# The last projection of a recurrent block in three fp32r passes on twelve of sixteen chunks, with low parts made by GpSimd

## What is computed

```
xn = layernorm(x)                                   # over the 256 values
A  = sigmoid(log_A);  Bx = xn @ B_w.T + B_b
h_t = A * h_(t-1) + Bx_t                            # along the 1024 tokens of a sequence
s  = h @ C_w.T + C_b
y  = sum over the top 2 of 8 experts of  c_e * (silu(xn @ W1_e) * (xn @ W3_e)) @ W2_e
out = x + s * silu(y)
```

## Time and profile before

| | |
|---|---|
| median of 3 runs | 799.54 us (797.96 to 799.91) |
| the profiled execution | 799.78 us, its span 798.0 us |
| PE busy | 771.4 us, 97% of the span |
| DVE, ACT, POOL busy | 518.2, 375.1, 463.8 us |
| share of the chain that ended last | PE 84%, DVE 8% |

### The profile page before, as it was taken

One profiled execution on the slowest core, in us unless ns is written; L12 is line 12 of the kernel. 1 busy time (PEld: TensorE's weight loads), 2 busy tenths in 40 slices (PEclk: granted clock), 3 DMA queues, 4 the chain that ended last, 5 costly groups with the idle time before them and its releaser, 6 DMA issues.

```text
span 798.0 us, 17126 instructions
## 1 busy us (share of the span) xinstructions
PE 771.4 (97%) x5399; PEld 688.8 (86%) x5399; DVE 518.2 (65%) x1083; ACT 375.1 (47%) x665; POOL 463.8 (58%) x477
## 2 busy tenths in 40 slices
PE   4999989999999999999999999999999999999997
PEld 2554449999999999999999999999999999998786
DVE  6988965676777667666866564455556765552766
ACT  3975234454455345444544553445445654442530
POOL 4742847687476766856783687476547856544000
PEclk9999999999999999999999999999999999999999
DMA  9999913544565545435543644363537555943994
GB/s 291 330 302 334 131 41 107 125 77 67 127 141 113 101 81 106 68 53 135 138 70 96 165 61 79 42 145 60 112 67 192 98 128 101 329 66 40 307 373 165
DMA packets 101842, 111.02 MB, mean 139 GB/s; under 512 B 15634, under 2 KB 89236, under 8 KB 101748
## 3 DMA queue, kind: packets, MB, share of 16 engines
q0 software_dynamic: 25920, 35.54, 27.4%
q1 hardware_dynamic: 50032, 50.34, 20.3%
q10 hardware_dynamic: 25796, 24.20, 10.4%
HBM read 66.61 MB, written 43.45 MB: 138 GB/s over the span
## 4 chain that ended last, share of the span: by engine, by line
PE 84%; DVE 8%; DMA 2%; issue 2%; ACT 2%; ACTq 0%; POOL 0%; DVEq 0%; POOLq 0%; SPq 0%
PE bank L1506 15%; PE bank L1505 15%; PE bank L1507 15%; PE bank L1531 15%; PE bank L1532 7%; PE bank L1638 6%; PE bank L1494 3%; DVE xnT L1084 3%; PE bank L1406 2%; DVE stats L955 1%; PE bank L1369 1%; DVE xnT L1096 1%; PE bank L1557 1%; PE bank L1558 1%; PE bank L1556 1%
## 5 line engine op out<-in xcount | busy, mean ns | idle before, releaser
L605 POOL DMA_INDIRECT y_rows<-y_sb,token_at x128 | 215.5, 1684 | 150.8 <-DVE y_sb L1202 84.4
L1505 PE MATMUL bank<-xh,W_sb 128*128 128x256 f32 x1008 | 283.1, 281 | 1.2 <-DVE xl L1150 1.2
L1506 PE MATMUL bank<-xh,W_sb 128*128 128x256 f32 x1008 | 281.8, 280 | 0.0
L1507 PE MATMUL bank<-xl,W_sb 128*128 128x256 f32 x1008 | 281.7, 279 | 0.0
L1505 PEld LDWEIGHTS bank<-xh,W_sb 128*128 128x128 f32 x1008 | 189.2, 188 | 3.4 <-issue 1.3
L1531 PE MATMUL bank<-W_sb,hh 128*128 128x512 f32 x512 | 189.0, 408 | 0.7 <-DVE y_sb L1202 0.7
L1506 PEld LDWEIGHTS bank<-xh,W_sb 128*128 128x128 f32 x1008 | 189.4, 188 | 0.0
L1507 PEld LDWEIGHTS bank<-xl,W_sb 128*128 128x128 f32 x1008 | 188.9, 187 | 0.0
L1190 DVE TENSOR_TENSOR hbuf<-hbuf,bank 128x512 f32<-128x512 f32 x128 | 87.3, 686 | 148.8 <-PE bank L1507 129.5
L596 POOL DMA_INDIRECT xg<-xn_rows,token_at x128 | 145.3, 1136 | 37.8 <-issue 18.3
L1532 PE MATMUL bank<-W_sb,hl 128*128 128x256 f32 x512 | 143.9, 281 | 0.0
(11 more groups left out here) (253 smaller groups left out, 939.1 us busy)
## 6 DMA issues: line engine op xcount, KB each, us to landing
x_late<-L_attn_x SPq DMA_DIRECT2D x24, 512.0 KB, 9.2
raw<-L_ffn_W ACTq DMA_DIRECT2D x24, 512.0 KB
odd_raw<-L_ffn_W ACTq DMA_DIRECT2D x21, 512.0 KB
xn_rows<-h_sb SPq DMA_DIRECT2D x16, 512.0 KB, 7.4
y_rows<-xnT SPq DMA_DIRECT2D x4, 2048.0 KB, 16.2
yy<-y_rows SPq DMA_DIRECT2D x16, 512.0 KB, 9.3
out<-x_late SPq DMA_DIRECT2D x11, 512.0 KB, 6.6
x_kept<-L_attn_x SPq DMA_DIRECT2D x4, 512.0 KB, 6.9
```

What stands on the lines that cost most here:

```text
L605: return eng.indirect_dma_start(out=y_rows, out_offset=rows, in_=y, in_offset=None, bounds_check=T + TW - 1, oob_is_err=True, compute_op=A ...
L1505: eng.matmul(part, high, x_h, start=k == 0, stop=False)
L1506: eng.matmul(part, low, x_h, start=False, stop=False)
L1507: last = eng.matmul(part, high, x_l, start=False, stop=k == KD - 1)
```

## The change

Chunks 4 to 15 (`SPLIT_FROM` = 4) no longer use f32 matmuls. Their states are split in a part rounded to fp32r (`h_high`) and the rest (`h_low`), and so is the matrix (`CwT_high`, `CwT_low`); three fp32r matmuls of 256 columns (high by high, high by low, low by high) take the place of each f32 matmul. `h_high`, `h_low` and `h_sb` share one stretch of SBUF: the high part of chunk c is written where the states of chunk c-4 stood, so it waits until `states_out(c-4)` is done; the low part is written over the chunk's own states. ACT makes the high parts (Copy, 128 x 1024), POOL the low parts (a subtract, 128 x 1024, after its last scatter), DVE the low part of the matrix. On ACT the high parts of chunks 4, 5 and 6 stand ahead of the first silu, that of 7 behind the silu of chunk 0, and those of 8 to 15 behind the silus of 4 to 11. The load of the first chunk of y and its silu are cut in two halves.

```diff
+        with ExitStack() as split:
+            h_high = sb("h_high", [P, BATCH * KN * SEQ], f32r, split)
+        with ExitStack() as split:
+            h_low = sb("h_low", [P, BATCH * KN * SEQ], f32r, split)
         h_sb = sb("h_sb", [P, BATCH * KN * SEQ], f32)
...
+        SPLIT_FROM = len(S_BANKS)
+        def split_home(c):
+            home = c - SPLIT_FROM
+            return h_half(home // 2 * 2, home % 2, h_high)
...
             for c in range(CHUNKS):
-                eng.dma_start(yy[:, c, :].rearrange("p (t d) -> p t d", t=CT), y_v[:, c * CT:(c + 1) * CT, :]).then_inc(y_loaded[c], 16)
+                yy_c, y_c = yy[:, c, :].rearrange("p (t d) -> p t d", t=CT), y_v[:, c * CT:(c + 1) * CT, :]
+                if c == 0:
+                    eng.dma_start(yy_c[:, 0:2, :], y_c[:, 0:2, :]).then_inc(y_first_half, 16)
+                    eng.dma_start(yy_c[:, 2:4, :], y_c[:, 2:4, :]).then_inc(y_loaded[c], 16)
+                else:
+                    eng.dma_start(yy_c, y_c).then_inc(y_loaded[c], 16)
...
+            for c in range(SPLIT_FROM, CHUNKS):
+                eng.wait_ge(hs_high, c - SPLIT_FROM + 1)
+                eng.tensor_tensor(h_half(c // 2 * 2, c % 2, h_low), h_half(c // 2 * 2, c % 2), split_home(c).bitcast(f32),
+                                  ALU.subtract).then_inc(hs_low, 1)
...
+            def split(c):
+                eng.wait_ge(s_psum, 2 * (c - SPLIT_FROM) + 2)
+                eng.activation(split_home(c), h_half(c // 2 * 2, c % 2), ACT.Copy).then_inc(hs_high, 1)
+            eng.wait_ge(CwT_ready, 1)
+            eng.activation(CwT_high[:, :], CwT[:, :], ACT.Copy).then_inc(CwT_high_ready, 1)
+            for c in range(SPLIT_FROM, 2 * SPLIT_FROM - 1):
+                split(c)
             for c in range(CHUNKS):
-                eng.wait_ge(y_loaded[c], 16)
-                eng.activation(yy[:, c, :], yy[:, c, :], ACT.Silu).then_inc(g_ready, 1)
+                if c == 0:
+                    eng.wait_ge(y_first_half, 16)
+                    eng.activation(yy[:, c, 0:512], yy[:, c, 0:512], ACT.Silu).then_inc(g_ready, 1)
+                    eng.wait_ge(y_loaded[c], 16)
+                    eng.activation(yy[:, c, 512:1024], yy[:, c, 512:1024], ACT.Silu).then_inc(g_ready, 1)
+                    split(2 * SPLIT_FROM - 1)
+                else:
+                    eng.wait_ge(y_loaded[c], 16)
+                    eng.activation(yy[:, c, :], yy[:, c, :], ACT.Silu).then_inc(g_ready, 1)
+                if SPLIT_FROM <= c < CHUNKS - SPLIT_FROM:
+                    split(c + SPLIT_FROM)
...
+            eng.wait_ge(CwT_high_ready, 1)
+            eng.tensor_tensor(CwT_low[:, :], CwT[:, :], CwT_high[:, :].bitcast(f32), ALU.subtract).then_inc(CwT_low_ready, 1)
...
+                if c >= SPLIT_FROM:
+                    if c == SPLIT_FROM:
+                        eng.wait_ge(CwT_low_ready, 1)
+                    eng.wait_ge(hs_low, c - SPLIT_FROM + 1)
...
+                            else:
+                                high, low = split_home(c)[:, m, tokens], h_half(c // 2 * 2, c % 2, h_low)[:, m, tokens]
+                                eng.matmul(o, high, CwT_high[:, of], start=False, stop=False)
+                                eng.matmul(o, high, CwT_low[:, of], start=False, stop=False)
+                                last = eng.matmul(o, low, CwT_high[:, of], start=False, stop=ends and m == KN - 1)
```

More of the change, by code:

```diff
@@ L147, in build @@
             CwT = sb("CwT", [P, KN * D], f32, tail)
-            pad_to_weights = sb("pad_to_weights", [P, W_COLS - 2 * KN * D - 3 * D - P], f32, tail)
+            CwT_high = sb("CwT_high", [P, KN * D], f32r, tail)
+            CwT_low = sb("CwT_low", [P, KN * D], f32r, tail)
+            pad_to_weights = sb("pad_to_weights", [P, W_COLS - 4 * KN * D - 3 * D - P], f32, tail)
             yy = sb("yy", [P, CHUNKS, CT * D], f32, tail)
@@ L311, in build, with h_half @@
         y_loaded = [sem(f"y_loaded{c}") for c in range(CHUNKS)]
+        y_first_half = sem("y_first_half")
         s_psum = sem("s_psum")
+        CwT_high_ready, CwT_low_ready = sem("CwT_high_ready"), sem("CwT_low_ready")
+        hs_high, hs_low = sem("hs_high"), sem("hs_low")
         g_ready, u_ready, out_ready = sem("g_ready"), sem("u_ready"), sem("out_ready")
         out_stored = sem("out_stored")
-        def h_half(g0, q):
-            return h_sb[:, bass.ds(g0 * SEQ, KN * SEQ)].rearrange("p (m s) -> p m s", m=KN)[:, :, q * CW:(q + 1) * CW]
+        def h_half(g0, q, of=h_sb):
+            return of[:, bass.ds(g0 * SEQ, KN * SEQ)].rearrange("p (m s) -> p m s", m=KN)[:, :, q * CW:(q + 1) * CW]
+        SPLIT_FROM = len(S_BANKS)
+        def split_home(c):
+            home = c - SPLIT_FROM
+            return h_half(home // 2 * 2, home % 2, h_high)
         def wait_apart(eng, semaphore, value):
@@ L1334, in add_x @@
                 eng.tensor_tensor(x_g, yy[:, c, at:at + cols], x_g, ALU.add).then_inc(out_ready, 1)
+            eng.wait_ge(CwT_high_ready, 1)
+            eng.tensor_tensor(CwT_low[:, :], CwT[:, :], CwT_high[:, :].bitcast(f32), ALU.subtract).then_inc(CwT_low_ready, 1)
             for c in range(CHUNKS - 1):
-                eng.wait_ge(g_ready, c + 1)
+                eng.wait_ge(g_ready, c + 2 if c else 1)
                 apply(c, 0, 512, S_BANKS[c % 4][0], 2 * c + 1)
@@ L1340, in _ @@
                     add_x(c - 1, 512, 512, 2 * c)
+                else:
+                    eng.wait_ge(g_ready, 2)
                 apply(c, 512, 512, S_BANKS[c % 4][1], 2 * c + 2)
@@ L1343, in _ @@
             c = CHUNKS - 1
-            eng.wait_ge(g_ready, CHUNKS)
+            eng.wait_ge(g_ready, CHUNKS + 1)
             for n, (at, cols, b) in enumerate(LAST_PARTS):
@@ L1635, in states_out @@
                     for t in range(at // D, (at + cols) // D):
-                        o = bank[b][:, t * D - at:(t + 1) * D - at]
+                        o, tokens, ends = bank[b][:, t * D - at:(t + 1) * D - at], slice(t * P, (t + 1) * P), (t + 1) * D == at + cols
                         for m in range(KN):
-                            last = eng.matmul(o, h_g[:, m, t * P:(t + 1) * P], CwT[:, m * D:(m + 1) * D],
-                                              start=False, stop=(t + 1) * D == at + cols and m == KN - 1)
+                            of = slice(m * D, (m + 1) * D)
+                            if c < SPLIT_FROM:
+                                last = eng.matmul(o, h_g[:, m, tokens], CwT[:, of], start=False, stop=ends and m == KN - 1)
+                            else:
+                                high, low = split_home(c)[:, m, tokens], h_half(c // 2 * 2, c % 2, h_low)[:, m, tokens]
+                                eng.matmul(o, high, CwT_high[:, of], start=False, stop=False)
+                                eng.matmul(o, high, CwT_low[:, of], start=False, stop=False)
+                                last = eng.matmul(o, low, CwT_high[:, of], start=False, stop=ends and m == KN - 1)
                     last.then_inc(s_psum, 1)
```

## The result

| kernel | median of its runs | lowest to highest | runs | profiled execution (its span) |
|---|---|---|---|---|
| before | 799.39 us | 796.79 to 800.37 | 20 | 799.78 (798.0) |
| after | 800.56 us | 798.13 to 801.60 | 20 | 798.61 (796.9) |

A forecast was written before the change was run, and what follows sets the result against it. PE was taken to bound the kernel before, DVE after: DVE's end without waits at 782.65 plus 14.1 us of holds, 1.4 us later than before, gave 801.0 us against 799.54; 8-in-10 range 790.5 to 805.5.

The forecast's parts named there:

- Half chunk on PE: PE in chunks 4 to 15: four fp32r triplets and a bias, 1.65 us for 1.97, saving 7.6 us of PE.
- First chunk in halves: First chunk of y: PE starts chunk 4 1.25 us earlier; the clock's fall taken as gone, some 1.9 us.
- the sum: DVE's operations and holds added up over the tail: apply of chunk 1 at 745.75, DVE's end at 796.75.
- Copy on ACT: ACT's high parts: a 128x1024 copy takes 1.1 us, hidden behind PE; chunk 7's copy moves silu 1 to 744.65.
- POOL's hold: POOL's low parts: each subtract of 1024 elements keeps DVE's adds with two SBUF inputs out for 2.2 us.
- The added waits: DVE's adds: 0.7 for chunk 7's low part, 1.6 each for 8 to 11, 1.75 each for 12 to 15; 14.1 us.
- DVE's end: End of the tail: 782.65 without waits plus 14.1 of holds is 796.75, against 795.34 before, 1.4 us later.
- Rival 1: DVE and POOL hardly disturb each other, holds of 0.2 us; late output stores set the end, 792 us; chance 0.27.
- Rivals 2 and 3: Rival 2: POOL holds longer, 806 us, chance 0.12; rival 3: the clock stays down as PE waits, 810 us, chance 0.03.

The follow-up runs named there:

- chunks 4 to 7 in passes: Changed kernel with three passes in chunks 4 to 7 alone, low parts by POOL, chunks 8 to 15 in f32; 793.93 us, 0.9942 of before.
- halves only: Kernel before with the first chunk of y loaded and put through silu in two halves, f32 in all chunks; 796.06 us, 0.9970 of before.
- passes only: Changed kernel with the first chunk of y whole, as before, everything else kept; 802.74 us, 1.0062 of before.
- the version that only writes low parts: Changed kernel with POOL's subtract replaced by a memset of zeros, so low parts aren't computed; 791.29 us, 0.9896 of before.
- Low part in quarters: Changed kernel with each low part as four POOL subtracts of 256 columns; 795.18 us, 0.9959 of before.

## Why the prediction was right

- **Half chunk on PE, 1.65.** 1.63 measured (779.02 to 780.65). The passes' gain alone is seen where nothing holds adds: chunks 4 to 7 in passes are 2.1 us under halves only (793.93 to 796.06, before being 0.3 slower in that batch), expected 2.6.
- **First chunk in halves.** (In after PE isn't the bound, so of these terms only the earlier start of DVE counts in the sum.) PE was to start chunk 4 1.25 us earlier. It starts it 4.2 us after the load begins, before 5.9: 1.65 earlier. The clock didn't fall at this place in after or in halves only. It didn't fall in passes only either, though PE stood for 2 us there as before; so it isn't shown that the halves are what spared the fall. Together the two were sized at 3.2 us; halves only measured 2.4 (0.3%). A likely reason: before doesn't lose the same amount to the clock each time. Its executions beside the experiments had mean granted clocks from 0.992 to 0.999, the three at 0.999 took 795.7 to 796.4 us, those at 0.995 took 798.5 to 800.7, and the one profiled, with its fall near 746, had 0.995. In how many of the others the clock fell at that place isn't shown.
- **Copy on ACT, 1.1.** The high parts take 1.04 to 1.06 and what waits for them is POOL, whose low parts come early enough: PE's side waited for one once, 0.8 us. Their cost was to be 0.25 at silu 1. Silu 1 was late for another reason that I hadn't priced: y's second chunk landed and silu 1 began at 742.77, 6.4 us after the load began, in place of 5.5. Two issues of SP stood ahead of it (0.37, 0.47 in the chain) in place of one, so it was issued 0.94 us after the load began (737.33 - 736.39). Only some 0.5 us of the 0.9 can be that, and in the version that only writes low parts, with the same two issues, the chunk landed after 5.5: why it came late isn't shown. Apply of chunk 1 began 7.5 us after the load started, not 6.9.
- **POOL's hold, 2.2 us for 1024.** 2.28 measured from one's end to the other's. The Trainium skill (GPSIMD Engine Reference, "Elementwise — side-by-side cycle accounting") has 4497 ns for a tensor_tensor of 2048 elements; half of it, an estimated 2.25 us, agrees.
- **The added waits, 14.1 us.** 13.2: eight adds, seven at 1.6 and one at 1.96. The terms were mis-sized in both directions: for the low part of 7 I had 0.7, and no add met it, since DVE waited for y's second chunk (idle 2.11) while POOL computed; for 12 to 15 I had 1.75, and three of the four were 1.6.
- **DVE's end.** 39.1 us of work, 2.1 of waiting for y and 13.2 of holds are the 54.4 from the first apply to the last add's end. That end lies 57.8 us after the load's start, before 56.5; +1.3 where the sum had +1.4. So close a hit is in part luck: the apply of chunk 1 came 0.6 later than in the sum and the waits were 0.9 shorter, and the two nearly cancel. PE, as foreseen, waits for applies (5.7 us in 8 waits) and was done at 787.2. The prediction's reading that every entry of before's chain is PE up to 793.7 was wrong (791.77); its sum doesn't use it.
- **Rival 1 (792)** needed POOL not to disturb DVE. It is the version that only writes low parts: 791.3. Its arithmetic was right, its condition wasn't given., on which it rested, are of an operation with one tensor input, and those hold for less.
- **Rivals 2 and 3** did not come: the hold was under 2.35 us, and the clock kept its upper level while PE stood for about 0.7 us at a time. Low part in quarters, in which PE stood up to 2.3 us at a time, did show the lower level, 0.50 from 750 to 752; passes only, where it stood 2.2, did not. All this is of one execution each. After's profiled one had a mean clock of 0.997; 15 of its 20 executions had 0.991 to 0.995 and took 799.5 to 801.6 us, so the clock fell more often in them, and where isn't shown.

The Trainium skill (SBUF — State Buffer, "SBUF: two separate sides") has the port pair exclusive between a DVE operation with two SBUF inputs and a GpSimd operation that reads SBUF, for the whole instruction. The runs agree for POOL's tensor_tensor, whose hold of 2.28 us reaches to its end, and for its memset, which reads nothing and held nothing. For the one-input tensor_scalar they differ: 0.98 us of 2.77.

## What to carry to other kernels

Before work is moved from VectorE to GpSimd, or given to it beside a busy VectorE, price what it holds: count VectorE's operations with two SBUF inputs that will meet it, and compare the hold with what VectorE would need to do the work itself (here 1.6 against 1.13 us). A change that brings a gain and a loss of the same size looks like no change; run each part alone, and try the number of units between none and all, since here four to eight of twelve chunks gave 0.6 to 0.8% where twelve gave nothing. Put such work where the other engine waits anyway: in after and in the version with four, the first four low parts held no add. The margin was small: in passes only the fourth held an add to 2.74 us.

## What the hardware showed that I had not expected

- One-input POOL operations keep adds out for 0.55 us (512 elements) and 0.98 us (1024) from their issue, though they take 1.49 and 2.77 us. Two-input ones keep them out to their end. It may be the time in which POOL reads, but only lengths were measured; what is held isn't shown.
- On POOL an f32 tensor_scalar of 1024 elements took longer (2.77 us) than a tensor_tensor with no add in its way (2.40 to 2.56).
- A waiting add isn't let in between POOL operations that follow each other without a gap: 3.64 us behind pieces of 512, 4.58 behind pieces of 256. Where adds already alternated with POOL, from 752 on in the same runs, they were let in after each of its operations; so they were in after, whose low parts of chunks 8 to 12 also followed each other without a gap, from 749.63 on. What decides between the two isn't settled.
- Applies, with one input in PSUM, took 0.67 to 0.69 beside POOL throughout.
